# Second layer of a two-layer model: which operands of the scan's side work lie in PSUM, and which engine adds an epsilon

## Chip, cores and metric

One core of a Trainium2 chip runs the whole program. The metric is device time in microseconds (us), the median of the runs. Engines are named as in the profile: PE multiplies matrices, DVE is the vector engine, ACT the scalar engine (functions by table), POOL the general one, and SP issues DMAs. Everything is float32.

## What is computed

The reference is a two-layer network on `x` of shape (4, 2048, 256). The first layer (an RWKV-like recurrence with a feed-forward part, then experts) is not touched. The second layer is a selective scan (Mamba-like) and then two groups of 32 experts, of which each token takes two in each group. Cut to what the change touches:

```python
# selective scan, d_inner = 512, d_state = 16, per token t (x here is layer-normalised)
x_ssm, res = split(x @ W_in.T)            # 512 and 512 columns
x_ssm = silu(conv4(x_ssm) + b_conv)
B_C   = x_ssm @ W_x.T                     # the second 16 columns
dt    = softplus(x_ssm @ W_dt.T + b_dt)   # the "step size"; its logits are x_ssm @ W_dt.T + b_dt
h     = exp(dt * A) * h + dt * B * x_ssm  # 512 x 16 states, one step per token
y     = (h.sum(-1) + D * x_ssm) * silu(res)
x     = x + y @ W_out.T
# experts, for each of two groups of 32 (on layernorm(x), eps 1e-5)
scores = softmax(xn @ router_w); w, idx = top_k(scores, 2)
out   += 0.5 * sum over the picks of w * expert[idx](xn)
```

## The kernel before

The 8192 tokens go through the second layer in 16 chunks of 512. `layer1_phase` (from L939) writes out one order of work for all engines. Its backbone is `scans` (L1341): 64 steps per chunk, one for each of 4 blocks `e` of 128 inner columns and each of 16 states `n`. In step `g`, POOL computes `dbx = dtx * B` for two states at a time (L1368), ACT computes `exp(A*dt)` into one of three PSUM banks (L1375), DVE runs the recurrence of step `g-2` over 512 tokens with one scan instruction (L1386, result `hs`), and PE transposes `hs` of step `g-3` and adds it up in PSUM (L1402). `dbx` has room for 6 steps and `hs` for 8.

After each step the loop pulls side work a little further (`background.pull`). The side work is written as generators: each `yield` ends a slot, and a stream advances by `rate` slots per step. Three streams run beside the scans of chunk `c`:

- `before(c + 1)`, rate 1.15: normalise (L998), transpose, input product, convolution (L1119), SiLU (L1128), gates (L1148), the product for B, and at the end `step_size(e)` for four blocks (L1164): PE makes the logits (L1167), ACT copies them with their bias into `dt` in SBUF (L1175) and makes `ln(1 + exp(-|z|))` in `tmp` (L1176, L1179, L1181), DVE adds `max(z, 0)` (L1184) and multiplies by `xs` to get `dtx` (L1188).
- `after_scan(c - 1)`, rate 1.15: transpose of the gated output, product with `W_out` in two halves, each with its sum into `xb` (L1233), normalise, transpose, `router` (L1457), then ranks and places of the picks (L1257 to L1308).
- `sort_rows(c - 1)`, rate 0.4: indirect DMAs that POOL issues (L1325).

Every engine runs its instructions in the order written. Three PSUM banks (`G = Banks(psum, 0, 3)`) serve both streams in turn; `claim` skips a bank whose last user has not yet been written out ("held"), and PE waits for the mark in `G.freed` before it writes the bank again.

`normalise` takes mean and variance on DVE (L1003, L1006), adds the epsilon on DVE (L1008), raises to -0.5 on POOL (L1011), and makes the shift on DVE (L1014):

```python
m = dve.mark(nc.vector.tensor_scalar(rstd[:, :], mv[:, :, 1], EPS_LN, None, ALU.add))
yield from pause(POOL_LAG)
pool.after(m)
```

`router` handles 8 rows per partition (4 tiles, 2 groups) of 32 experts. ACT copies the scores from PSUM to `prob` (L1473); DVE takes the peak (L1478) and subtracts it (L1480); ACT applies exp (L1484); DVE sums (L1488), inverts (L1490), and divides all 256 values (L1492), picks the largest (L1496) and their indices (L1502), turns these to float (L1507), and compares them with `iota` into `onehot` (L1509), whose sum is `chosen` (L1513).

Of the kernel before, what the change touches and what calls it, by code (L numbers as in the profile page):

```python
# [5 lines left out]
P = 128  # L6
# [204 lines left out]
def layer0_phase(nc, psum, consts, I, L, sems, x_in, x_out, second_layer):  # L211
# [6 lines left out]
    with ExitStack() as st, ExitStack() as scanning:  # L218
# [51 lines left out]
        ssq, eps_gn, eps_rms = sb("ssq", [P, TL]), sb("eps_gn", [P, 1]), sb("eps_rms", [P, 1])  # L270
# [668 lines left out]
def layer1_phase(nc, psum, consts, I, L, sems, Z, route_of, x_in, x_out):  # L939
# [7 lines left out]
    with ExitStack() as st, ExitStack() as early:  # L947
# [6 lines left out]
        ident, neghalf = consts["ident"], consts["neghalf"]  # L954
# [120 lines left out]
        def before(c):  # L1075
# [88 lines left out]
            def step_size(e):  # L1164
# [19 lines left out]
                m = m_done["tmp free", e % 2] = m_done["dt", c, e] = dve.mark(nc.vector.scalar_tensor_tensor(  # L1184
                    out=dt_[:, e, :], in0=dt_[:, e, :], scalar=0.0, in1=tmp[:, e % 2, :], op0=ALU.max, op1=ALU.add))
# [19 lines left out]
        def after_scan(c):  # L1205
# [14 lines left out]
            dve.engine.wait_ge(s_xb, c * 16 + 16)  # L1220
            for half in range(2):
# [7 lines left out]
                m = pe.mark(m)  # L1229
                yield from pause(LAG)  # L1230
# [22 lines left out]
            dve.mark(nc.vector.tensor_scalar(route.weights[:, part, :].rearrange("p t (g k) -> p (t g) k", g=GR), R["best"][:, :, 0:TOP], 0.5, None, ALU.mult))  # L1253
# [203 lines left out]
def router(nc, L, G, xT, W_router, R, iota, groups, experts, top, lag=1):  # L1457

# [6 lines left out]
    rows = TL * groups  # L1465
    i, bank = yield from G.claim(pe)
# [11 lines left out]
    m = dve.mark(nc.vector.tensor_reduce(R["peak"][:, :], R["prob"][:, :, :], mybir.AxisListType.X, ALU.max))  # L1478
    dve.after(m)
    m = dve.mark(nc.vector.tensor_tensor(R["prob"][:, :, :], R["prob"][:, :, :], R["peak"][:, :].unsqueeze(2).broadcast_to([P, rows, experts]), ALU.subtract))  # L1480
    for _ in range(lag):
        yield
    act.after(m)
    m = act.mark(nc.scalar.activation(R["prob"][:, :, :], R["prob"][:, :, :], ACT.Exp))  # L1484
    for _ in range(lag):
        yield
    dve.after(m)
    m = dve.mark(nc.vector.tensor_reduce(R["total"][:, :], R["prob"][:, :, :], mybir.AxisListType.X, ALU.add))  # L1488
    dve.after(m)
    m = dve.mark(nc.vector.reciprocal(R["total"][:, :], R["total"][:, :]))  # L1490
    dve.after(m)
    m = dve.mark(nc.vector.tensor_tensor(R["prob"][:, :, :], R["prob"][:, :, :], R["total"][:, :].unsqueeze(2).broadcast_to([P, rows, experts]), ALU.mult))  # L1492
    yield
# [13 lines left out]
    m = dve.mark(nc.vector.tensor_copy(R["index_f"][:, :, :], R["index"][:, :, 0:top]))  # L1507
    dve.after(m)
    m = dve.mark(nc.vector.tensor_tensor(R["onehot"][:, :, :, :], iota[:, 0:experts].unsqueeze(1).unsqueeze(1).broadcast_to([P, rows, top, experts]),  # L1509
                                         R["index_f"][:, :, :].unsqueeze(3).broadcast_to([P, rows, top, experts]), ALU.is_equal))  # L1510
# [537 lines left out]
```

## Time and profile before

| | |
|---|---|
| median of 3 runs | 5326.36 us (5324.19 to 5327.82) |
| profiled execution | 5320.49 us, of which its span 5318.7 us |
| mean granted TensorE clock | 0.918 of full |
| busy over the span | PE 84%, DVE 74%, POOL 57%, ACT 49% |
| second layer with its scans | about 2680 to 4600 us of the span |

The span is the time from the first to the last instruction. A "group" below is all instructions of one line and form; behind its count stand the busy us of the group and the mean ns of one, then the idle us of the engine just before them and who ended it.

### The profile page before, as it was taken

Reading aid. Unit: us, or ns where it says so; the run is one execution under the profiler, and the core shown is the slowest. Engines: PE = TensorE matmul, PEld = TensorE weight load, DVE = VectorE, ACT = ScalarE, POOL = GpSimd, SP = SyncE. Lnnn points to the kernel's source line nnn. Section 1 sums busy time; section 2 is a strip of 40 time slices with the busy share of each in tenths; the row PEclk is TensorE's granted clock in tenths of the full one; section 3 lists DMA queues with packets and bytes.
Section 4 is the critical chain, followed back from the end, with each engine's and each line's share of the span. In section 5 each row is a group of like instructions: output and inputs, shape, how many; then the busy total and the mean of one; then the engine's idle time right before and its main releaser. Section 6 shows DMA issues by size and latency. Waiting matters only on the chain.

```text
span 5318.7 us, 58348 instructions
## 1 busy us (share of the span) xinstructions
PE 4466.3 (84%) x18832; PEld 2897.8 (54%) x18832; DVE 3946.1 (74%) x6263; ACT 2597.7 (49%) x4829; POOL 3016.0 (57%) x1940
## 2 busy tenths in 40 slices
PE   4788989888898888899978888888888888489994
PEld 1344555555555555566655555555555555378773
DVE  5977677676776767675078998898999888645676
ACT  1244344434433444444566666666666666244442
POOL 2445444445543445453167778777777777645552
PEclk8799999999999999999988899989988898699997
DMA  3223232323332233332121111111212111386777
GB/s 120 88 99 101 91 99 84 97 86 103 107 97 76 91 96 95 101 102 84 48 81 52 68 60 60 60 60 61 77 70 72 61 61 62 146 235 195 240 247 266
DMA packets 302654, 545.49 MB, mean 103 GB/s; under 512 B 30736, under 2 KB 146704, under 8 KB 293392
## 3 DMA queue, kind: packets, MB, share of 16 engines
q1 hardware_dynamic: 274704, 466.10, 27.0%
q0 software_dynamic: 27648, 75.67, 3.9%
q8 instruction: 153, 2.51, 0.2%
q14 instruction: 149, 1.22, 0.1%
HBM read 422.73 MB, written 118.92 MB: 102 GB/s over the span
## 4 chain that ended last, share of the span: by engine, by line
PE 50%; DVE 25%; ACT 9%; issue 7%; POOL 6%; DMA 2%; SPq 0%; DVEq 0%; POOLq 0%; another core or an unknown queue 0%; ACTq 0%
PE psum L207 21%; DVE c_hs L1386 7%; PE psum L1856 5%; PE psum L762 5%; DVE a_S L857 4%; PE psum L646 4%; POOL c_dbx L1368 4%; PE psum L1119 4%; PE psum L1402 3%; DVE a_prod L863 3%; PE psum L1879 3%; PE psum L1841 1%; PE psum L879 1%; ACT L770 1%; POOL sorted_rows L1325 1%
## 5 line engine op out<-in xcount | busy, mean ns | idle before, releaser
L1368 POOL TENSOR_TENSOR c_dbx<-c_dtx,c_Brep 128x1024 f32<-128x1024 f32 x512 | 1211.5, 2377 | 399.9 <-DVE c_hs L1386 328.0
L848 POOL TENSOR_TENSOR a_kv<-a_rk,a_kv 128x512 f32<-128x512 f32 x512 | 764.8, 1507 | 564.5 <-DMA a_kv<-v_rows 564.3
L1386 DVE TENSOR_TENSOR_SCAN c_hs<-psum,c_carry,c_dbx 128x512 f32<-128x512 f32 x768 | 931.6, 1262 | 47.2 <-ACT psum L1375 40.5
L1375 ACT ACTIVATE psum<-c_dt,c_cols 128x512 f32<-128x512 f32 x1024 | 698.2, 689 | 473.1 <-DVE c_hs L1386 469.3
L1402 PE MATMUL psum<-ident,c_hs 128*128 128x128 f32 x4096 | 703.1, 311 | 261.6 <-DVE c_hs L1386 252.5
L781 POOL TENSOR_TENSOR a_hid_e<-a_hid_e,a_g_rep 128x512 f32<-128x512 f32 x256 | 381.4, 1493 | 825.5 <-ACT a_hid_e L770 617.8
L1402 PEld LDWEIGHTS psum<-ident,c_hs 128*128 128x128 f32 x4096 | 540.8, 159 | 557.3 <-DVE c_hs L1386 395.0
L857 DVE TENSOR_TENSOR_SCAN a_S<-a_decay,a_carry,a_kv 128x513 f32<-128x513 f32 x512 | 785.7, 1535 | 38.7 <-POOL a_kv L848 33.9
L207 PE MATMUL psum<-a_xT,a_W_up 128*128 128x512 f32 x1152 | 579.6, 634 | 67.1 <-ACT a_hid_e L770 66.8
L863 DVE TENSOR_TENSOR a_prod<-a_rk,a_S 128x512 f32<-128x512 f32 x512 | 513.9, 1004 | 124.9 <-PE psum L879 124.8
L762 PE MATMUL psum<-a_W_down,a_hid_e 128*128 128x256 f32 x2304 | 552.4, 385 | 17.0 <-POOL a_hid_e L781 17.0
L762 PEld LDWEIGHTS psum<-a_W_down,a_hid_e 128*128 128x128 f32 x2304 | 438.7, 193 | 199.0 <-issue 108.1
L1768 POOL DMA_INDIRECT results<-d_ys,d_to_row x320 | 312.4, 976 | 276.5 <-issue 121.8
L207 PEld LDWEIGHTS psum<-a_xT,a_W_up 128*128 128x128 f32 x1152 | 222.8, 200 | 292.8 <-issue 186.4
L770 ACT ACTIVATE a_hid_e<-psum 128x512 f32<-128x512 f32 x288 | 170.5, 596 | 360.9 <-PE psum L207 359.9
L1856 PE MATMUL psum<-d_w,d_xT 128*128 x1280 | 333.8, 384 | 3.6 <-issue 3.1
L1386 DVE TENSOR_TENSOR_SCAN c_hs<-psum,c_dbx 128x512 f32<-128x512 f32 x256 | 295.0, 1201 | 34.8 <-ACT psum L1375 27.1
L1325 POOL DMA_INDIRECT sorted_rows<-route_xn,route_to_row x256 | 269.8, 1054 | 63.1 <-issue 45.5
L207 PE MATMUL psum<-a_xT,a_w 128*128 128x256 f32 x1024 | 248.4, 390 | 13.4 <-ACT a_hid_f L654 11.9
L1167 PE MATMUL psum<-c_xs,c_W_dt 128*128 128x512 f32 x512 | 246.8, 606 | 0.0
L646 PE MATMUL psum<-a_w,a_hid_f 128*128 128x256 f32 x1024 | 240.6, 381 | 4.7 <-ACT a_hid_f L654 4.7
L1871 DVE TENSOR_TENSOR d_h<-d_h,psum 128x128 f32<-128x128 f32 x320 | 91.8, 287 | 205.0 <-ACT d_h L1867 145.8
(265 smaller groups left out, 7343.0 us busy)
## 6 DMA issues: line engine op xcount, KB each, us to landing
a_kv<-v_rows SPq DMA_DIRECT2D x512, 256.0 KB
a_g_rep<-g_rows SPq DMA_DIRECT2D x256, 256.0 KB, 3.7
c_Brep<-b_rows SPq DMA_DIRECT2D x64, 1024.0 KB, 4.7
d_xs<-sorted_rows SPq DMA_DIRECT2D x320, 128.5 KB
d_w<-results SPq DMA_DIRECT2D x64, 512.0 KB, 11.5
d_w<-in_d_experts SPq DMA_DIRECT2D x32, 768.0 KB
sorted_rows<-d_zeros SPq DMA_DIRECT2D x66, 128.5 KB, 3.8
a_xa<-in_L_attn_x SPq DMA_DIRECT2D x16, 512.0 KB, 4.7
```

Of the source, the lines that this page charges most:

```text
L207: last = nc.tensor.matmul(out, lhsT, rhs, start=(n == 0), stop=(n == len(pairs) - 1))
L646: m_down = nc.tensor.matmul(sums[:, t * D:(t + 1) * D], hid_f[:, r, s * HALF + t * P:s * HALF + (t + 1) * P], w2[:, 2 * (f - 1) + s, :], s ...
L762: m_down = nc.tensor.matmul(banks[t // 2][1][:, (t % 2) * D:(t % 2 + 1) * D], hid_e[:, r, t * P:(t + 1) * P], W_down[:, q, :], start=(q == ...
L781: hid[e - 1] = m_done["gate used", n] = pool.mark(nc.gpsimd.tensor_tensor(hid_e[:, r, :], hid_e[:, r, :], g_rep[:, n % NG, :], ALU.mult))
L848: m_kv[g] = pool.mark(nc.gpsimd.tensor_tensor(kv[:, g % NV, 1:C + 1], rk[slot][:, 1, hb, :], kv[:, g % NV, 1:C + 1], ALU.mult))
L857: m_scan[q] = dve.mark(nc.vector.tensor_tensor_scan(S[:, q % NS, :], decay[cq % 2][:, hb, :], kv[:, q % NV, :], carry[:, sq_:sq_ + 1], ALU ...
L863: m_prod[q] = dve.mark(nc.vector.tensor_tensor(prod[:, q % NP, :], rk[cq % 2][:, 0, sq_ // DK, :], S[:, q % NS, 0:C], ALU.mult))
L1368: m_dbx[g] = m_dbx[g + 1] = pool.mark(nc.gpsimd.tensor_tensor(dbx[:, r:r + 2, :], dtx[slot][:, e, :].unsqueeze(1).broadcast_to([P, 2, C]), ...
L1375: m_da[g] = act.mark(nc.scalar.activation(psum[:, DA + g % ND, :], dt[slot][:, e, :], ACT.Exp, scale=A[:, e, n:n + 1]))
L1386: m_scan[q] = dve.mark(nc.vector.tensor_tensor_scan(hs[:, q % NR, :], psum[:, DA + q % ND, :], dbx[:, q % NX, :], first, ALU.mult, ALU.add))
L1402: last = nc.tensor.matmul(psum[:, YB + e % 2, t * P:(t + 1) * P], hs[:, q % NR, t * P:(t + 1) * P], ident[:, :], is_transpose=True, start= ...
L1856: m = nc.tensor.matmul(bank[:, 0:2 * P], xT[:, q % N3, kb * P:(kb + 1) * P], w[:, bass.ds(at_w[q] + kb * 2 * P, 2 * P)], start=(kb == 0), ...
```

## The change

Six edits, all but the first two inside `before`, `after_scan` and `router`:

1. A constant tile `eps` is shared by both layers (the first layer's `eps_gn` becomes this tile; what it holds is the same).
2. In the second layer's `normalise`, ACT adds the epsilon instead of DVE, two slots after the variance; POOL's power comes one slot later than before.
3. The step logits with their bias stay in their PSUM bank (ACT rewrites them there, after the absolute value) until DVE reads them for the sum; the bank is free after that sum and not after ACT's second reading.
4. In `router`, there is no copy by ACT: DVE reads the scores from the PSUM bank. The probabilities are not divided by their sum; the weights of the picks are multiplied by the inverse sum instead. The indices of the picks are written as floats into the same bank beside the scores, and the one-hot comparison reads them there. The bank is free after that comparison.
5. The two products with `W_out` are issued in two banks, and both sums follow.
6. The wait for `xb` moves from before the products to before the sums.

```diff
@@ normalise
-            dve.after(m)
-            m = dve.mark(nc.vector.tensor_scalar(rstd[:, :], mv[:, :, 1], EPS_LN, None, ALU.add))
-            yield from pause(POOL_LAG)
+            yield from pause(LAG)
+            act.after(m)
+            m = act.mark(nc.scalar.activation(rstd[:, :], mv[:, :, 1], ACT.Identity, bias=eps[:, 0:1]))
+            yield from pause(POOL_LAG - 1)
@@ step_size
-                m_z = act.mark(nc.scalar.activation(dt_[:, e, :], bank, ACT.Identity, bias=b_dt[:, e, :]))
-                m = G.freed[i] = act.mark(nc.scalar.activation(tmp[:, e % 2, :], bank, ACT.Abs, bias=b_dt[:, e, :]))
+                act.mark(nc.scalar.activation(tmp[:, e % 2, :], bank, ACT.Abs, bias=b_dt[:, e, :]))
+                m = m_z = act.mark(nc.scalar.activation(bank, bank, ACT.Identity, bias=b_dt[:, e, :]))
...
-                m = m_done["tmp free", e % 2] = m_done["dt", c, e] = dve.mark(nc.vector.scalar_tensor_tensor(
-                    out=dt_[:, e, :], in0=dt_[:, e, :], scalar=0.0, in1=tmp[:, e % 2, :], op0=ALU.max, op1=ALU.add))
+                dve.after(*scanned)
+                m = G.freed[i] = m_done["tmp free", e % 2] = m_done["dt", c, e] = dve.mark(nc.vector.scalar_tensor_tensor(
+                    out=dt_[:, e, :], in0=bank, scalar=0.0, in1=tmp[:, e % 2, :], op0=ALU.max, op1=ALU.add))
@@ after_scan
-            dve.engine.wait_ge(s_xb, c * 16 + 16)
+            products = []
             for half in range(2):
                 i, bank = yield from G.claim(pe)
...
-                m = pe.mark(m)
-                yield from pause(LAG)
+                products.append((i, bank, pe.mark(m)))
+                yield
+            yield from pause(LAG)
+            dve.engine.wait_ge(s_xb, c * 16 + 16)
+            for half, (i, bank, m) in enumerate(products):
                 dve.after(m)
...
-            dve.mark(nc.vector.tensor_scalar(route.weights..., R["best"][:, :, 0:TOP], 0.5, None, ALU.mult))
+            dve.after(m)
+            dve.mark(nc.vector.scalar_tensor_tensor(out=route.weights..., in0=R["best"][:, :, 0:TOP], scalar=0.5,
+                                                    in1=R["total"][:, :].unsqueeze(2).broadcast_to([P, TL * GR, TOP]), op0=ALU.mult, op1=ALU.mult))
@@ router
-    for _ in range(lag - 1):
+    scores = bank[:, 0:TL * NE].rearrange("p (r e) -> p r e", e=experts)
+    picks = bank[:, TL * NE:TL * NE + rows * top].rearrange("p (r k) -> p r k", k=top)
+    for _ in range(lag + 1):
         yield
-    act.after(m)
-    m = act.mark(nc.scalar.copy(R["prob"]..., bank[:, 0:TL * NE]))
-    G.freed[i] = m
-    for _ in range(lag):
-        yield
     dve.after(m)
-    m = dve.mark(nc.vector.tensor_reduce(R["peak"], R["prob"], X, ALU.max))
+    m = dve.mark(nc.vector.tensor_reduce(R["peak"], scores, X, ALU.max))
     dve.after(m)
-    m = dve.mark(nc.vector.tensor_tensor(R["prob"], R["prob"], R["peak"] broadcast, ALU.subtract))
+    m = dve.mark(nc.vector.tensor_tensor(prob, scores, R["peak"] broadcast, ALU.subtract))
...
-    m = dve.mark(nc.vector.reciprocal(R["total"], R["total"]))
-    dve.after(m)
-    m = dve.mark(nc.vector.tensor_tensor(R["prob"], R["prob"], R["total"] broadcast, ALU.mult))
-    yield
-    dve.after_alone(m)
...
-    m = dve.mark(nc.vector.tensor_copy(R["index_f"], R["index"][:, :, 0:top]))
-    dve.after(m)
-    m = dve.mark(nc.vector.tensor_tensor(R["onehot"], iota broadcast, R["index_f"] broadcast, ALU.is_equal))
+    m = dve.mark(nc.vector.tensor_copy(picks, R["index"][:, :, 0:top]))
+    dve.mark(nc.vector.tensor_copy(R["index_f"], R["index"][:, :, 0:top]))
+    dve.mark(nc.vector.reciprocal(R["total"], R["total"]))
+    dve.after(m)
+    m = G.freed[i] = dve.mark(nc.vector.tensor_tensor(R["onehot"], iota broadcast, picks broadcast, ALU.is_equal))
```

(The indices of some views are shortened here. In `router` the instructions for the largest values now follow the sum in its slot.)

## Rows read from the trace of the kernel before

**Rows 1.** Timeline of DVE, first and last of 12 one-hot comparisons: start, length (us)
```profile
2857.14 2.89 DVE L1509 TENSOR_TENSOR c_onehot<-c_iota,c_index_f 128x512 f32<-128x512 f32 x1
...
4192.21 2.90 DVE L1509 TENSOR_TENSOR c_onehot<-c_iota,c_index_f 128x512 f32<-128x512 f32 x1
```

**Rows 2.** Windows view: stretch, length, busy us of each engine, TensorE clock, DMA
```profile
3225.00:3289.00 64.00, 47.03 (x234) 32.06 (x233) 63.12 (x71) 41.08 (x74) 48.50 (x26) 0.89 0.24 91
3289.00:3326.00 37.00, 36.94 (x176) 23.88 (x175) 29.37 (x33) 21.96 (x38) 35.05 (x19) 1.00 0.14 47
3326.00:3344.00 18.00, 16.42 (x62) 8.09 (x61) 13.95 (x38) 15.87 (x23) 10.27 (x7) 0.91 0.05 18
```

**Rows 3.** Chain of waits in one chunk: start us, length us, what
```profile
3285.07 0.66 PE psum L1402 x4
...
3324.33 1.75 PE psum L207 x16
...
3326.10 0.37 ACT c_prob L1473
...
3327.78 1.26 ACT c_xs L1128 x2
```

**Rows 4.** Groups of DVE instructions, 2450 to 4600 us
```profile
L1184 DVE SCALAR_TENSOR_TENSOR c_dt<-c_dt,c_tmp 128x512 f32<-128x512 f32 x64 | 83.4, 1302 | 42.8 <-ACT c_tmp L1181 42.7
L1188 DVE TENSOR_TENSOR c_dtx<-c_dt,c_xs 128x512 f32<-128x512 f32 x64 | 71.9, 1124 | 1.1
L1014 DVE SCALAR_TENSOR_TENSOR c_shift<-c_mv,c_rstd 128x4 f32<-128x4 f32 x31 | 46.6, 1502 | 1.1 <-POOL c_rstd L1011 1.1
...
L1509 DVE TENSOR_TENSOR c_onehot<-c_iota,c_index_f 128x512 f32<-128x512 f32 x15 | 39.4, 2624 | 0.5
L1008 DVE TENSOR_SCALAR c_rstd<-c_mv 128x4 f32<-128x4 f32 x31 | 36.8, 1186 | 1.1
L1492 DVE TENSOR_TENSOR c_prob<-c_prob,c_total 128x256 f32<-128x256 f32 x15 | 30.3, 2021 | 0.5
...
L1233 DVE TENSOR_TENSOR c_xb<-c_xb,psum 128x512 f32<-128x512 f32 x30 | 20.6, 687 | 40.0 <-PE psum L207 40.0
...
L1480 DVE TENSOR_TENSOR c_prob<-c_prob,c_peak 128x256 f32<-128x256 f32 x15 | 16.4, 1092 | 0.5
...
L1304 DVE SCALAR_TENSOR_TENSOR c_place<-c_index_f,c_place 128x16 f32<-128x16 f32 x15 | 9.2, 614 | 0.5
...
L1478 DVE TENSOR_REDUCE c_peak<-c_prob 128x8 f32<-128x256 f32 x15 | 6.3, 418 | 59.4 <-ACT c_prob L1473 59.4
```

**Rows 5.** Timeline of POOL, then of DVE, where the one-hot comparison starts
```profile
3344.29 2.34 POOL L1368 TENSOR_TENSOR c_dbx<-c_dtx,c_Brep 128x1024 f32<-128x1024 f32 x1 [0.25 <-DVE c_index_f L1507]
...
3344.30 2.88 DVE L1509 TENSOR_TENSOR c_onehot<-c_iota,c_index_f 128x512 f32<-128x512 f32 x1
```

**Rows 6.** Timeline of DVE at the step sizes of one chunk
```profile
3357.74 0.73 DVE L1184 SCALAR_TENSOR_TENSOR c_dt<-c_dt,c_tmp 128x512 f32<-128x512 f32 x1
...
3371.29 2.47 DVE L1184 SCALAR_TENSOR_TENSOR c_dt<-c_dt,c_tmp 128x512 f32<-128x512 f32 x1
3373.80 0.69 DVE L1188 TENSOR_TENSOR c_dtx<-c_dt,c_xs 128x512 f32<-128x512 f32 x1
...
3377.95 1.89 DVE L1184 SCALAR_TENSOR_TENSOR c_dt<-c_dt,c_tmp 128x512 f32<-128x512 f32 x1
```

**Rows 7.** Timeline of PE, then of DVE, behind the router's product
```profile
3328.52 5.40 PE L207 MATMUL psum<-c_W_in,c_xT 128*128 128x512 f32 x8 [1.58 <-ACT c_xs L1128]
...
3331.08 3.63 DVE L1386 TENSOR_TENSOR_SCAN c_hs<-psum,c_carry,c_dbx 128x512 f32<-128x512 f32 x3 [2.51 <-ACT psum L1375]
```

**Rows 8.** Groups of ACT instructions, 2450 to 4600 us
```profile
L1375 ACT ACTIVATE psum<-c_dt,c_cols 128x512 f32<-128x512 f32 x1024 | 698.2, 689 | 473.1 <-DVE c_hs L1386 469.3 <-issue 1.3
...
L332 ACT ACTIVATE a_rstd<-a_mv,a_eps_gn 128x4 f32<-128x4 f32 x1 | 0.3, 297 | 0.0
```

**Rows 9.** Timeline of PE at the third step-size product
```profile
3356.87 1.88 PE L1167 MATMUL psum<-c_xs,c_W_dt 128*128 128x512 f32 x4
```

More of the change, by code:

```diff
@@ L269, in layer0_phase @@
         ln_rstd, ln_shift = small("ln_rstd"), small("ln_shift")
-        ssq, eps_gn, eps_rms = sb("ssq", [P, TL]), sb("eps_gn", [P, 1]), sb("eps_rms", [P, 1])
+        ssq, eps_gn, eps_rms = sb("ssq", [P, TL]), consts["eps"], sb("eps_rms", [P, 1])
         R = router_buffers(nc, st, "a", 1, E, TOP)
@@ L953, in layer1_phase @@
         s_load, s_rest, s_xa, s_xb, s_store, s_bout = (sem(n) for n in ("load", "rest", "xa", "xb", "store", "bout"))
-        ident, neghalf = consts["ident"], consts["neghalf"]
+        ident, neghalf, eps = consts["ident"], consts["neghalf"], consts["eps"]
         norm = [None, None]
@@ L1252, in after_scan @@
             dve.mark(nc.vector.tensor_scalar(xn_[:, :, D], token_row[:, :], float(c * C * TOP), None, ALU.add))
-            dve.mark(nc.vector.tensor_scalar(route.weights[:, part, :].rearrange("p t (g k) -> p (t g) k", g=GR), R["best"][:, :, 0:TOP], 0.5, None, ALU.mult))
+            dve.after(m)
+            dve.mark(nc.vector.scalar_tensor_tensor(out=route.weights[:, part, :].rearrange("p t (g k) -> p (t g) k", g=GR), in0=R["best"][:, :, 0:TOP], scalar=0.5,
+                                                    in1=R["total"][:, :].unsqueeze(2).broadcast_to([P, TL * GR, TOP]), op0=ALU.mult, op1=ALU.mult))
             ahead = route.ahead
@@ L1465, in router @@
     rows = TL * groups
+    prob, best = R["prob"], R["best"]
     i, bank = yield from G.claim(pe)
@@ L1469, in router @@
     m = pe.mark(m)
-    for _ in range(lag - 1):
+    scores = bank[:, 0:TL * NE].rearrange("p (r e) -> p r e", e=experts)
+    picks = bank[:, TL * NE:TL * NE + rows * top].rearrange("p (r k) -> p r k", k=top)
+    for _ in range(lag + 1):
+        yield
+    dve.after(m)
+    m = dve.mark(nc.vector.tensor_reduce(R["peak"][:, :], scores, mybir.AxisListType.X, ALU.max))
+    dve.after(m)
+    m = dve.mark(nc.vector.tensor_tensor(prob[:, :, :], scores, R["peak"][:, :].unsqueeze(2).broadcast_to([P, rows, experts]), ALU.subtract))
+    for _ in range(lag):
         yield
     act.after(m)
-    m = act.mark(nc.scalar.copy(R["prob"][:, :, :].rearrange("p r e -> p (r e)"), bank[:, 0:TL * NE]))
-    G.freed[i] = m
+    m = act.mark(nc.scalar.activation(prob[:, :, :], prob[:, :, :], ACT.Exp))
     for _ in range(lag):
@@ L1477, in router @@
     dve.after(m)
-    m = dve.mark(nc.vector.tensor_reduce(R["peak"][:, :], R["prob"][:, :, :], mybir.AxisListType.X, ALU.max))
-    dve.after(m)
-    m = dve.mark(nc.vector.tensor_tensor(R["prob"][:, :, :], R["prob"][:, :, :], R["peak"][:, :].unsqueeze(2).broadcast_to([P, rows, experts]), ALU.subtract))
-    for _ in range(lag):
-        yield
-    act.after(m)
-    m = act.mark(nc.scalar.activation(R["prob"][:, :, :], R["prob"][:, :, :], ACT.Exp))
-    for _ in range(lag):
-        yield
-    dve.after(m)
[L1488 to L1493, printed above, removed]
-    dve.after_alone(m)
+    m_total = dve.mark(nc.vector.tensor_reduce(R["total"][:, :], prob[:, :, :], mybir.AxisListType.X, ALU.add))
     for r in range(rows):
-        m = dve.mark(nc.vector.max(R["best"][:, r, :], R["prob"][:, r, :]))
+        m = dve.mark(nc.vector.max(best[:, r, :], prob[:, r, :]))
         if r == rows // 2 - 1:
@@ L1501, in router @@
     for r in range(rows):
-        m = dve.mark(nc.vector.max_index(R["index"][:, r, :], R["best"][:, r, :], R["prob"][:, r, :]))
+        m = dve.mark(nc.vector.max_index(R["index"][:, r, :], best[:, r, :], prob[:, r, :]))
         if r == rows // 2 - 1:
@@ L1505, in router @@
     yield
+    dve.after(m, m_total)
+    m = dve.mark(nc.vector.tensor_copy(picks, R["index"][:, :, 0:top]))
+    dve.mark(nc.vector.tensor_copy(R["index_f"][:, :, :], R["index"][:, :, 0:top]))
+    dve.mark(nc.vector.reciprocal(R["total"][:, :], R["total"][:, :]))
     dve.after(m)
[L1507 to L1510, printed above, removed]
+    m = G.freed[i] = dve.mark(nc.vector.tensor_tensor(R["onehot"][:, :, :, :], iota[:, 0:experts].unsqueeze(1).unsqueeze(1).broadcast_to([P, rows, top, experts]),
+                                                      picks.unsqueeze(3).broadcast_to([P, rows, top, experts]), ALU.is_equal))
     dve.after(m)
@@ L1927, in build @@
         consts = {"ident": st.enter_context(nc.sbuf_tensor("ident", [P, P], F32)),
+                  "eps": st.enter_context(nc.sbuf_tensor("eps", [P, 1], F32)),
                   "neghalf": st.enter_context(nc.sbuf_tensor("neghalf", [P, 4], F32))}
```

## The prediction

> **What bounds the kernel now.** I read the page's slices first: the second layer shows a DVE that is nearly always busy, beside a PE that is hardly less so. To part the two I took the timeline of DVE and looked for an instruction that comes once per chunk. The one-hot comparison does; 12 of them span 11 chunks, (4192.21 - 2857.14) / 11 = 121.4 us each [rows 1]. Then I cut one chunk with the windows view [rows 2]. It has three stages, and each has another limit:
>
> - A, 64 us, from the one-hot comparison to the first sum into `xb`: DVE is busy 63.12 of 64, PE 47.03. DVE sets the time here.
> - B, 37 us, up to the router's product: PE is busy 36.94 of 37, DVE 29.37. PE sets the time, and what DVE saves here is worth nothing.
> - C, 18 us, up to the next comparison: no engine is full (PE 16.42, ACT 15.87, DVE 13.95). The three wait for each other.
>
> The chain of waits agrees: from 3285.07 it runs over PE to the end of the router's product at 3326.08, goes over to ACT's copy of the scores (3326.10, 0.37 us) and from there to the SiLU that stands behind this copy in ACT's order [rows 3]. DVE's peak (L1478) stood 59.4 us in 15 chunks waiting for that copy [rows 4].
>
> Then I read DVE's groups for instructions that take longer than their size [rows 4]. A 128x512 sum with one operand in PSUM (L1233) takes 687 ns. The comparison has the same size and both operands in SBUF, and takes 2624. L1184 takes 1302, L1188 1124, the division L1492 2021, and L1008 1186 for four columns. The timeline shows why: POOL starts a `dbx` at 3344.29 that lasts to 3346.63, the comparison starts 0.01 us later and lasts 2.88, so that it ends 0.55 us after POOL [rows 5]. It stood while POOL ran. The 30 sums with a PSUM operand average 0.687, so they show no such wait.
>
> The Trainium skill (SBUF — State Buffer, section Who interferes with whom) states this as a lock: a DVE instruction with two SBUF inputs, or one in a two-port mode, and a GpSimd instruction that reads SBUF exclude each other for the whole instruction. The trace agrees, with 2.88 against 0.69 us. The same rule speaks against the change at one place: L1188 keeps two SBUF inputs, so it can inherit what L1184 no longer waits. If all four step sizes passed it on, that edit would bring nothing, and the sum below would be 1.2 us per chunk (18 us in all) smaller.
>
> **The change, part by part**, in us per chunk; 15 chunk times carry both side streams.
>
> One-hot comparison: 2.62 falls to 0.69, the row of a PSUM operand: 1.93. Behind it stand a scan, a reduction and short work, about 2.6 us, by which time the `dbx` has ended. All of it lies in A and counts.
>
> Epsilon of the incoming chunk: L1008 leaves DVE in A, 1.19. ACT gets the nearest row's 0.30 [rows 8]; ACT stands idle 473 us before its exponentials in this stretch, which hides it. Were ACT full it would cost 2 x 0.30. The variance is written two slots ahead, so nothing is queued behind a wait; POOL's power comes a slot later, and `before` has some 68 of 73.6 slots filled, so it still ends in time. The second epsilon (for `xb`) lies in B: nothing.
>
> Step sizes: 4 x (1.30 - 0.69) = 2.44 of waiting in L1184, all in A. Where `dtx` follows directly, it takes the wait over: at 3371.29 L1184 took 2.47 and L1188 behind it 0.69 [rows 6]. Where a scan lies between, as after 3377.95, POOL has ended. The bounds are 0 and 2.44; the rows show about one of each kind, so I take half, 1.22. ACT's rewriting into PSUM costs what its PSUM-writing exponentials do, 0.69 [rows 8], the size of the instruction it replaces: nothing.
>
> Router, entry (C): ACT no longer stands behind the scores. Its SiLU and exponentials run while PE works. PE waited 1.58 for that SiLU at 3328.52, and DVE 2.51 for the exponential at 3331.08 [rows 7]. The lower bound is 1.58. The upper is 2.51 + 0.37, when DVE and not PE sets C. I take PE's 1.58 and the copy's 0.37, 1.95, since PE is the fuller engine in C.
>
> Router, division: L1492 (2.02) and the wait in L1480 (1.09 - 0.42, by the peak's row of the same size: 0.67) go. Between 0 and 2.69; C has other limits than DVE, so I take 0.
>
> Output halves: DVE's 40 us of waiting in L1233, 1.33 each, lie where PE is full. They go, and nothing comes of it. The wait for `xb` moves with them; its load is issued before the transposes, so it is covered as before.
>
> Added on DVE: a second copy of the indices, and weights with two SBUF inputs. The nearest row is L1304 (128x16, two SBUF inputs), 0.61 with its waits. Each is between nothing and 0.61; I take 0.4 for both, and at most 1.2.
>
> Banks: the router holds one of three for 11 slots, and each step size holds one until DVE's sum. The third step size would take the first one's bank: PE began it at 3356.87 [rows 9], while L1184 of the first ran from 3357.74 to 3358.47 [rows 6]. That is 1.6 of waiting, in A, where PE has 17 us of idle time. I take 0; the bound is 1.6.
>
> Sum: A 1.93 + 1.19 + 1.22 = 4.34; C 1.95; less 0.4; 5.9 per chunk, times 15 = 88 us. From the profiled 5320.5 that makes 5232; the median of the runs shown lies 5.9 above the profiled execution: **5238**. Low end: 1.93 + 1.19 + 0 + 1.58 - 1.2 - 1.6 = 1.9, 28 us. High end: 1.93 + 1.19 + 2.44 + 2.88 + 2.69 = 11.1, 167 us.
>
> **Rivals.**
>
> 1. The waiting is handed on. L1188 or L1014 (1502 ns for four columns [rows 4]) stands against POOL instead, or scans come up against `dbx`, since DVE and POOL then both run dense. POOL's 48.50 of 64 in A speaks against the latter; rows 6 speak for the former in part. A then keeps only about half of the one-hot and epsilon parts, 1.6, and C its 1.95, less 0.4: 3.1, or 47 us, 5279.
> 2. C becomes DVE's own. With ACT ahead and the division gone, 1.2 of the 2.69 counts, C gives 2.3 in place of 1.95, and the step sizes pass on nothing: 5.9 + 1.2 + 0.35 + 1.22 = 8.7 per chunk, 130 us, 5196. For it: DVE idles 2.51 beside PE's 1.58. Against: PE has only 1.6 us of room in C.
> 3. PE bounds the whole chunk. It is busy about 100 of 121 us, and the granted clock is 0.89 in A against 1.00 in B [rows 2]; if what A gives is lost again at the clock, the time stays at 5326. Against: PE has 17 us of idle time in A.
> 4. Slower: two banks do not suffice. The place is B and C, where PE is full: the gate and B products must then wait for ACT's evacuation of a bank that it used one or two products ago. One such wait costs about the 1.58 of rows 7. It decides from four per chunk (5.9 / 1.58); with five, 8 us, the change costs 2 per chunk, 32 us, 5358. Against: the SiLU that frees each bank is no longer held up by the scores.
>
> **How the numbers follow.** Forecast 0.52 (own range 5215 to 5262), rival 1 0.22, rival 2 0.14, rival 3 0.05, rival 4 0.07. A measurement of this kernel can tell about 0.2%, some 11 us. Faster is the first three, 0.88; the same 0.05; slower 0.07. The range 5185 to 5300 leaves out rivals 3 and 4 and the far ends of 1 and 2, about 0.18 together.
>
> **What the profile would show.** The comparison near 0.69 us, L1184's successor near 0.69 in all 64, its `dtx` between 0.7 and 1.7 on average; a chunk time near 115.5; stage B still 37 us; a peak that waits for PE and not for ACT; no PE idle time at the gates' product. Wrong would be shown by PE waits on DVE's sum or on a SiLU in B or C, by a longer `dtx` group than 72 + 40 us of busy time, or by an unchanged A with shorter DVE instructions and more idle time on DVE.

## The result, and the profile after

The changed kernel takes 5201.66 us (median of 4 runs, 5199.28 to 5204.73) against 5325.27 before: ratio 0.9768, 95% interval 0.9753 to 0.9782. That is 124 us less, where 88 were forecast (5238 us). The time is also 13 us below the forecast's own range of 5215 to 5262, and nearest to the 5196 us of rival 2. Its profiled execution has a span of 5197.5 us.

The one-hot comparison marks the chunks as before. These are the first and the last of 12 in the timeline of DVE after the change (start, length):

```profile
2855.91 0.63 DVE L1508 TENSOR_TENSOR c_onehot<-c_iota,psum 128x512 f32<-128x512 f32 x1
...
4104.69 0.64 DVE L1508 TENSOR_TENSOR c_onehot<-c_iota,psum 128x512 f32<-128x512 f32 x1
```

(4104.69 - 2855.91) / 11 = 113.5 us per chunk, against 121.4 [rows 1]. So a chunk gives 7.8 us, and not 5.9. The comparison itself now takes 0.63 us in place of 2.89 (2.62 on average before).

The stages of one chunk in the windows view after (stretch, length, busy us of PE, PE's weight loads, DVE, ACT and POOL, TensorE clock, DMA share, GB/s), which answer to [rows 2]:

```profile
3196.00:3260.00 64.00, 53.21 (x253) 37.44 (x252) 62.42 (x75) 46.57 (x82) 53.40 (x28) 0.84 0.27 97
3260.00:3295.00 35.00, 33.48 (x164) 21.79 (x163) 30.23 (x31) 22.53 (x38) 30.20 (x16) 1.00 0.11 38
3295.00:3310.00 15.00, 14.59 (x65) 7.82 (x64) 11.87 (x35) 12.12 (x19) 10.29 (x7) 1.00 0.07 21
```

In A DVE is still the fullest (62.42 of 64), but PE has grown from 47.03 to 53.21 and POOL from 48.50 to 53.40. In B PE is no longer full: 33.48 of 35, where it was 36.94 of 37. C takes 15 us in place of 18 with PE at 14.59.

In A the granted clock has fallen from 0.89 to 0.84.

These windows are cut where one chunk happens to stand. A is 64 us long in both, in part because its end is the first sum into `xb`, and edit 5 has moved that sum behind both products: over 11 chunks it comes 65.8 us after the comparison in the kernel before, 64.6 in the changed one, and 62.8 in the changed one without edits 5 and 6 (u_halves, below). For the balance I averaged 11 chunks, by the starts of four instructions in the timeline of DVE:

| from ... to | before | after | difference |
|---|---|---|---|
| comparison ... statistics of the incoming chunk | 44.03 | 40.50 | -3.53 |
| ... statistics of `xb` | 29.63 | 28.01 | -1.62 |
| ... peak of the scores | 29.45 | 30.00 | +0.55 |
| ... next comparison | 18.26 | 15.01 | -3.25 |
| chunk | 121.37 | 113.52 | -7.85 |

The norm has one slot more and the router one fewer. So a scan has moved from the fourth part (8 scans before, 7 after) to the third, and these two are read together: -2.70. The first two, in which DVE is the fullest, give -5.15. In the third PE is still nearly full by these averages, busy for 29.4 of 30.0 us where it was 29.0 of 29.5; the 33.48 of 35 above is one chunk, and takes in the end of the second part.

The DVE groups after that answer to [rows 4], from 2450 to 4480 us, which again hold 15 routers, and the two new small instructions (L1259 the weights, L1504 the picks):

```profile
L1190 DVE TENSOR_TENSOR c_dtx<-c_dt,c_xs 128x512 f32<-128x512 f32 x64 | 82.1, 1282 | 0.1
L1015 DVE SCALAR_TENSOR_TENSOR c_shift<-c_mv,c_rstd 128x4 f32<-128x4 f32 x31 | 71.2, 2295 | 4.8 <-POOL c_rstd L1012 4.8
...
L1186 DVE SCALAR_TENSOR_TENSOR c_dt<-psum,c_tmp 128x512 f32<-128x512 f32 x64 | 42.4, 663 | 46.7 <-ACT c_tmp L1182 46.6
...
L1238 DVE TENSOR_TENSOR c_xb<-c_xb,psum 128x512 f32<-128x512 f32 x30 | 19.8, 672 | 17.7 <-PE psum L207 17.7
...
L1508 DVE TENSOR_TENSOR c_onehot<-c_iota,psum 128x512 f32<-128x512 f32 x15 | 9.5, 634 | 0.0
...
L1257 DVE TENSOR_SCALAR route_xn<-c_token_row 128x4 f32<-128x4 f32 x15 | 7.1, 474 | 0.0
L1483 DVE TENSOR_TENSOR c_prob<-psum,c_peak 128x256 f32<-128x256 f32 x15 | 6.4, 424 | 0.5
L1481 DVE TENSOR_REDUCE c_peak<-psum 128x8 f32<-128x256 f32 x15 | 6.3, 421 | 39.7 <-PE psum L207 39.7
...
L1311 DVE SCALAR_TENSOR_TENSOR c_place<-c_index_f,c_place 128x16 f32<-128x16 f32 x15 | 4.6, 307 | 0.5
...
L1259 DVE SCALAR_TENSOR_TENSOR route_weights<-c_best,c_total 128x16 f32<-128x16 f32 x15 | 2.7, 178 | 0.0
...
L1504 DVE CAST psum<-c_index 128x16 f32<-128x16 uint32 x15 | 2.4, 159 | 0.0
```

The sum of the step size (L1186) has the length of its size, 0.66 us, in all 64. But its product L1190 went from 1.12 to 1.28, and the shift L1015 from 1.50 to 2.30: part of the waiting was handed on. To see how much, take for the instructions that [rows 4] show to be longer than their size, and for the row numbers of the tokens (L1252 before), the busy time less its count times the shortest it can take (0.66 us for 128x512, 0.42 for 128x256, 0.15 to 0.17 for the small ones). I call this DVE's waiting, and take it from 2450 to 4600 us. It leaves out two small casts, of the indices and of the places, which wait as well: 1 and 2 us before, 2 and 2 after. Before it is 217 us (step sum 41, product 30, shift 42, comparison 30, epsilon 32, division 24, subtraction 10, places 7, token rows 3). After it is 113, of which 66 in the shift and 40 in the product.

Behind the router's product, the rows that answer to [rows 7], of PE, DVE and ACT in the timeline after:

```profile
3297.94 1.88 PE L207 MATMUL psum<-c_W_in,c_xT 128*128 128x512 f32 x4
...
3299.99 2.46 DVE L1393 TENSOR_TENSOR_SCAN c_hs<-psum,c_carry,c_dbx 128x512 f32<-128x512 f32 x2 [2.42 <-ACT psum L1382]
...
3297.27 0.69 ACT L1129 ACTIVATE c_xs<-psum,c_cols 128x512 f32<-128x512 f32 x1 [4.66 <-PE psum L1120]
3297.98 1.28 ACT L1382 ACT_TABLE_LOAD   x1
```

PE's gate product no longer waits (it stood 1.58 us). DVE still does, 2.42 us for an exponential. ACT stands ahead of that with a SiLU (L1129) that waits 4.66 us for the convolution, which PE now finishes only behind the router's product. Behind the SiLU ACT also loads a table for 1.28 us before the exponential can start. ACT was freed from one wait and met the next one.

### The profile page after: what moved, and what is told of

It reads as the page before. It is cut to its first block, busy times and chain, and to the rows that moved or that the text cites. A ratio compares the mean times of both kernels' runs of the same rounds, so it can differ in the third digit from the quotient of the medians.

```text
span 5197.5 us, 58292 instructions
## 1 busy us (share of the span) xinstructions
PE 4433.8 (85%) x18832; PEld 2891.8 (56%) x18832; DVE 3826.1 (74%) x6231; ACT 2617.9 (50%) x4859; POOL 3006.2 (58%) x1940
## 3 DMA queue, kind: packets, MB, share of 16 engines
q14 instruction: 149, 1.22, 0.1%
## 4 chain that ended last, share of the span: by engine, by line
PE 52%; DVE 20%; ACT 10%; POOL 8%; issue 6%; DMA 2%; SPq 0%; DVEq 0%; POOLq 0%; another core or an unknown queue 0%; ACTq 0%
PE psum L207 22%; POOL c_dbx L1375 5%; PE psum L1855 5%; PE psum L762 5%; DVE a_S L857 4%; DVE c_hs L1393 4%; PE psum L646 4%; PE psum L1120 4%; PE psum L1409 4%; DVE a_prod L863 3%; PE psum L1878 3%; PE psum L1840 2%; POOL sorted_rows L1332 1%; PE psum L879 1%; PE psum L1168 1%
## 5 line engine op out<-in xcount | busy, mean ns | idle before, releaser
L1409 PE MATMUL psum<-ident,c_hs 128*128 128x128 f32 x4096 | 686.1, 306 | 211.4 <-DVE c_hs L1393 206.1
L1409 PEld LDWEIGHTS psum<-ident,c_hs 128*128 128x128 f32 x4096 | 530.3, 156 | 480.9 <-DVE c_hs L1393 327.3
L207 PEld LDWEIGHTS psum<-a_xT,a_w 128*128 128x128 f32 x1024 | 200.0, 197 | 80.0 <-issue 23.3
```

Of the source, the lines that this page charges most:

```text
L207: last = nc.tensor.matmul(out, lhsT, rhs, start=(n == 0), stop=(n == len(pairs) - 1))
L1409: last = nc.tensor.matmul(psum[:, YB + e % 2, t * P:(t + 1) * P], hs[:, q % NR, t * P:(t + 1) * P], ident[:, :], is_transpose=True, start= ...
```

## The experiments

Four kernels are the one before with one part of the change alone, two split the router further, three take one edit of the full change back or away, one changes POOL's instruction size, and two go beyond the change. Each ratio is to the kernel before on the same chip. "Chunk" and "waiting" are read as above.

| kernel | ratio (95%) | chunk | DVE's waiting |
|---|---|---|---|
| before | 1 | 121.4 | 217 |
| p_step: edit 3 alone | 0.9945 (0.9932 to 0.9959) | 119.6 | 188 |
| p_router: edit 4 alone | 0.9902 (0.9886 to 0.9917) | 118.0 | 194 |
| r_scores: of edit 4, no copy by ACT | 0.9934 (0.9918 to 0.9949) | 118.7 | 208 |
| r_picks: of edit 4, picks in PSUM | 0.9953 (0.9940 to 0.9966) | 119.2 | 190 |
| p_eps: edit 2 alone | 1.0004 (0.9995 to 1.0014) | 122.0 | 165 |
| p_halves: edits 5 and 6 alone | 0.9951 (0.9938 to 0.9965) | 120.5 | 179 |
| full change | 0.9768 (0.9753 to 0.9782) | 113.5 | 113 |
| u_halves: full, edits 5 and 6 taken back | 0.9772 (0.9759 to 0.9785) | 112.9 | 101 |
| u_eps: full, edit 2 taken back | 0.9825 (0.9812 to 0.9837) | 116.0 | 118 |
| s_slot: u_eps with a slot more | 0.9817 (0.9803 to 0.9830) | 115.3 | 129 |
| x_single: before, POOL by single states | 0.9986 (0.9976 to 0.9996) | 121.6 | 192 |
| n_shift: full, shift off DVE | 0.9722 (0.9709 to 0.9736) | 111.7 | 47 |
| n_both: n_shift, step size in PSUM for dtx | 0.9683 (0.9670 to 0.9696) | 110.0 | 7 |

### Step logits in PSUM, alone (p_step)

The `step_size` part of the diff above, and nothing else.

> Before with edit 3 alone (step logits stay in PSUM until DVE's sum). Port theory (DVE with two SBUF inputs stands while POOL runs): the sum falls from 1.30 to 0.66 us in all 64, the product behind it takes over about a quarter of it, 1.8 us per chunk are left, 27 us: ratio 0.995. Rival (the wait is handed on whole to the product dtx): sum at 0.66, product from 1.12 to about 1.76 us, ratio 1.000. Rival (banks held longer stop PE): ratio above 1.002, PE waits on DVE's sum.

Its DVE groups, product and sum:

```profile
L1189 DVE TENSOR_TENSOR c_dtx<-c_dt,c_xs 128x512 f32<-128x512 f32 x64 | 81.6, 1275 | 1.1
...
L1185 DVE SCALAR_TENSOR_TENSOR c_dt<-psum,c_tmp 128x512 f32<-128x512 f32 x64 | 43.0, 672 | 42.8 <-ACT c_tmp L1181 42.7
```

The sum falls to 0.67. The product rises by 0.15, so that of the 40 us of waiting that the sums lost, 10 came back in it. 1.8 us per chunk are left, as expected here; the prediction had taken 1.22. That the rows of one chunk showed as many pairs that hand the wait on as pairs that don't made me take half; over all 64 it is a quarter. PE now waits for a bank until DVE's sum, 5.0 us in 5 waits between 2850 and 4100 us, where the prediction's bound was 1.6 per chunk; the ratio shows nothing of it.

### The router's edits, alone and split (p_router, r_scores, r_picks)

p_router has the whole `router` of the change and the new weights. r_scores takes only this of it:

```diff
-    m = act.mark(nc.scalar.copy(R["prob"][:, :, :].rearrange("p r e -> p (r e)"), bank[:, 0:TL * NE]))
-    G.freed[i] = m
...
-    m = dve.mark(nc.vector.tensor_tensor(R["prob"][:, :, :], R["prob"][:, :, :], R["peak"]...
+    m = G.freed[i] = dve.mark(nc.vector.tensor_tensor(R["prob"][:, :, :], scores, R["peak"]...
```

and r_picks only this:

```diff
-    G.freed[i] = m
...
+    m = dve.mark(nc.vector.tensor_copy(picks, R["index"][:, :, 0:top]))
...
+    m = G.freed[i] = dve.mark(nc.vector.tensor_tensor(R["onehot"]..., picks.unsqueeze(3)..., ALU.is_equal))
```

> Before with edit 4 alone (router: no copy by ACT, no division, picks in PSUM, weights with the inverse sum). Port theory with ACT freed from the copy: the comparison falls from 2.62 to 0.63 us (2.0 per chunk) and the stage between router and comparison gives 2 to 3 us: 4 to 5 us per chunk, 60 to 75 us, ratio 0.987. Rival (the gain comes only from DVE's shorter instructions in the DVE-bound stage): 30 us, ratio 0.994. Rival (the router's bank, held for 11 slots, costs PE): below 30 us, with PE waits on SiLU.

> Before with only the copy by ACT removed (DVE reads the scores from PSUM, the bank is free after the subtraction; division and comparison as before). My sum gives 1.95 us per chunk in the stage behind the router, 29 us, ratio 0.9945: no PE idle time before the gates' product. Rival (the gain of the router's edits is DVE's alone, from comparison and division): ratio 0.999 to 1.000.

> Before with only the comparison's picks in PSUM (a second small copy, the bank held until the comparison). The prediction's sum: comparison 2.62 to 0.63 us, 1.9 per chunk, 29 us, ratio 0.9945. Rival (handed on): the next instruction with a two-port mode or two SBUF inputs (the row numbers of the tokens, 0.36 us before, and the places, 0.61) takes it over, as both did in the router's edits together (1.68 and 1.85): 0 to 5 us, ratio 0.999 to 1.000.

p_router gave 52 us (0.0098 of 5317), less than expected. Its DVE groups show where the rest went, places, token rows and comparison:

```profile
L1306 DVE SCALAR_TENSOR_TENSOR c_place<-c_index_f,c_place 128x16 f32<-128x16 f32 x16 | 29.6, 1851 | 0.6
L1252 DVE TENSOR_SCALAR route_xn<-c_token_row 128x4 f32<-128x4 f32 x16 | 26.9, 1681 | 0.0
...
L1503 DVE TENSOR_TENSOR c_onehot<-c_iota,psum 128x512 f32<-128x512 f32 x16 | 10.2, 634 | 0.0
```

The comparison is free of its wait, but two instructions behind it, which stand against POOL like it, took it over: token rows from 0.36 to 1.68 us, places from 0.61 to 1.85. Together that is 42 us of new waiting.

Yet r_picks alone gave 25 us, and there token rows and places stayed at 0.37 and 0.61. So that the comparison's wait is handed on is no property of the edit. I take it to depend on where the streams stand against POOL when all edits of a kernel are in. In the full change token rows are at 0.47 and places at 0.31, and hardly anything is handed on at that place.

r_scores gave 35 us (0.0066 of 5283); the part between peak and comparison fell from 18.26 to 15.74. That is the step on ACT of the prediction, and somewhat more than its 1.95. In this kernel and in p_router PE no longer waits for the SiLU (15.8 us in 10 waits before, between 2850 and 4100 us), so the expected rivals, a gain of DVE's alone and a bank that costs PE, did not come true. The two parts add to 60 us, against 52 for the whole router. Dropping the division was not tried alone, and what it adds does not show beside what was handed on; the prediction had put it at 0.

### The epsilon (p_eps, u_eps, s_slot)

p_eps is the `normalise` part of the diff with the shared constant; u_eps is the full change without that part; s_slot is u_eps with one more slot:

```diff
-            yield from pause(POOL_LAG)
+            yield from pause(POOL_LAG + 1)
             pool.after(m)
```

> Before with edit 2 alone (ACT adds the epsilon of the second layer's norms; power and shift one slot later). Port theory as predicted: 1.19 us of the incoming chunk's norm count, 18 us, ratio 0.9965. Rival (the wait goes on to the shift, two SBUF inputs, 1.50 us before and 2.30 in the full change): shift above 2 us, ratio 0.999 to 1.000.

> The full change with the epsilon back on DVE (edit 2 taken back, slots as before). Alone it gave 1.0004. If its wait is handed on to the shift in any order of work: ratio 0.977 as in the full change, shift back near 1.5 us. Rival (it pays once the other edits have made DVE's order fixed): ratio 0.980.

> The full change with the epsilon back on DVE but the power one slot later, as with ACT's epsilon. Slot theory: what edit 2 brings in the full change (0.9768 against 0.9825 without it) is the slot, which puts other PE work ahead of the transposes that wait for ACT's normalised rows (19.8 us of PE waiting in ten chunks without it, none with it): ratio 0.978 to 0.979. Rival (it is the instruction taken off DVE, 1.16 us): ratio 0.982 to 0.983.

Alone the edit gave nothing, with the shift's group at

```profile
L1015 DVE SCALAR_TENSOR_TENSOR c_shift<-c_mv,c_rstd 128x4 f32<-128x4 f32 x31 | 61.2, 1973 | 5.3 <-POOL c_rstd L1012 5.1
```

that is 1.97 us in place of 1.50. This is less than the rival had named (above 2), and of the 32 us that the epsilon lost, the shift took 15 over. Still DVE's waiting as a whole fell by 52 us (44, if the cast of the indices is counted, which rose from 0.22 to 0.79 us), and the time did not follow. Much of that fall is in the router, where nothing was edited: the division went from 2.02 to 0.60 us, and the comparison is at

```profile
L1510 DVE TENSOR_TENSOR c_onehot<-c_iota,c_index_f 128x512 f32<-128x512 f32 x15 | 10.4, 693 | 0.5
```

PE's waits between 2850 and 4100 us show two that grew (waiting instruction and who ended it: us, times, longest):

```profile
PE psum L207 <- DVE route_ahead L1261: 24.2, 11, 2.2
PE psum L207 <- ACT c_xs L1129: 22.2, 11, 2.0
```

The wait for `route_ahead` was not in that list before at all, and the one for `c_xs` was 15.8. But the largest, for `hs`, fell from 148.8 to 119.6, and all in the list together from 183 to 170. What grew is PE's busy time: from 2680 to 4560 us it is 1609 us against 1582, with about as many matmuls (7323 against 7336) and at a lower granted clock (0.87 against 0.89). So it is PE's longer work and not its waiting that stands against DVE's gain. Why it was longer was not tried.

In the full change the same edit is worth 0.9825 - 0.9768 = 0.0057, 30 us. My first thought was the slot that comes with it, since without the edit PE stands before the transposes of the normalised rows (same view, u_eps):

```profile
PE psum L1036 <- ACT route_xn L1018: 19.8, 10, 3.4
```

s_slot has the slot without the edit. That wait is gone from its list, and the ratio is 0.9817, within the interval of u_eps. The slot theory falls. What was on record as its rival, the instruction taken off DVE, is left. s_slot and the full change have the same slots and differ in the epsilon's engine, and by the averages over 11 chunks the second part of the chunk goes from 28.82 to 28.01 and the third from 31.00 to 30.00, with the other two unchanged. So both epsilons count, the one for `xb` too. In the third part PE is busy for 29.8 of 31.0 us in s_slot and 29.4 of 30.0 in the full change: with the epsilon on DVE it had 1.2 us of room there.

### Both halves, then both sums (p_halves, u_halves)

The `after_scan` part of the diff alone, and the full change without it.

> Before with edits 5 and 6 alone (both output products, then both sums, the wait for xb behind the products). As predicted: DVE's waits of 1.33 us at the sums lie where PE is full, so ratio 1.000 although these waits shrink. Rival (they count: up to 2.7 us per chunk, 40 us): ratio 0.992.

> The full change with edits 5 and 6 taken back (each output half with its sum at once). Alone these edits gave 0.9951, against my step that DVE's waits at the sums cost nothing because PE is full there. Theory of PE order: what counts is that the second product need not stand behind DVE's first sum in the slot order, so that PE and the norm start earlier; taking it back costs about 25 us here too, ratio 0.981 to 0.982. Rival, phase: alone the edits only moved DVE's two-input instructions against POOL's (the comparison fell to 0.69 us without PSUM), which PSUM operands already give in the full change; then the ratio stays at 0.977 to 0.978.

The prediction had said that nothing comes of this edit. Alone it gives 26 us. Its DVE groups, token rows and comparison:

```profile
L1255 DVE TENSOR_SCALAR route_xn<-c_token_row 128x4 f32<-128x4 f32 x15 | 28.8, 1920 | 0.0
...
L1512 DVE TENSOR_TENSOR c_onehot<-c_iota,c_index_f 128x512 f32<-128x512 f32 x15 | 10.4, 692 | 0.5
```

The comparison reads SBUF as before and takes 0.69 us: the other order has moved it away from POOL's instructions. The token rows took 1.6 us of that over. The division lost its wait in the same way (2.02 to 0.62). DVE's waits at the sums fell too, from 40.0 to 19.5 us. Against that PE stands at the transposes of the normalised rows (waits of p_halves, 2850 to 4100 us):

```profile
PE psum L1036 <- ACT route_xn L1018: 18.6, 10, 3.4
```

In the full change the edit is worth nothing: 0.9772 without it and 0.9768 with it. This is what the rival on phase had said, that the gain alone came at places that operands in PSUM make safe anyway. It is argued and not shown, and p_eps speaks against a simple form of it: there too the comparison (0.69) and the division (0.60) lost their waits and the token rows took some over (1.85), and nothing was gained. The chunk average gives 0.9 us, or 14 of the 26; the rest lies outside the 11 chunks. How much of the gain came from the comparison and how much from the sums is not settled.

### POOL's instruction half as long (x_single)

```diff
-                        m_dbx[g] = m_dbx[g + 1] = pool.mark(nc.gpsimd.tensor_tensor(
-                            dbx[:, r:r + 2, :], dtx[slot][:, e, :].unsqueeze(1).broadcast_to([P, 2, C]), Brep[:, n:n + 2, :], ALU.mult))
+                        for k in range(2):
+                            m_dbx[g + k] = pool.mark(nc.gpsimd.tensor_tensor(
+                                dbx[:, r + k:r + k + 1, :], dtx[slot][:, e, :].unsqueeze(1).broadcast_to([P, 1, C]), Brep[:, n + k:n + k + 1, :], ALU.mult))
```

> Before with POOL's product dbx issued for one state at a time (two instructions of 512 columns for one of 1024; the work is the same). Port theory: DVE's two-input instructions stand until the POOL instruction under way has ended, so halving that instruction about halves the excess: comparison from 2.62 to about 1.7 us, the sum of the step size from 1.30 to about 1.0, shift from 1.50 to about 0.9. Rival (the excess is the SBUF operand's own slowness): these stay as they were. The time: DVE gains up to 6 us per chunk, POOL pays two starts for one; between 0.985 and 1.01.

DVE's step sum, shift and comparison, then POOL's group:

```profile
L1184 DVE SCALAR_TENSOR_TENSOR c_dt<-c_dt,c_tmp 128x512 f32<-128x512 f32 x64 | 65.6, 1025 | 42.7 <-ACT c_tmp L1181 42.6
L1014 DVE SCALAR_TENSOR_TENSOR c_shift<-c_mv,c_rstd 128x4 f32<-128x4 f32 x31 | 45.5, 1469 | 9.2 <-POOL c_rstd L1011 9.2
...
L1510 DVE TENSOR_TENSOR c_onehot<-c_iota,c_index_f 128x512 f32<-128x512 f32 x15 | 28.5, 1900 | 0.5
```

```profile
L1369 POOL TENSOR_TENSOR c_dbx<-c_dtx,c_Brep 128x512 f32<-128x512 f32 x1024 | 1302.4, 1302 | 305.2 <-DVE c_hs L1387 241.4 <-DVE c_best L1497 26.0 <-DMA c_Brep<-b_rows 17.0
```

The comparison went from 2.62 to 1.90 and the step sum from 1.30 to 1.03, though nothing was changed at them or their operands. The excess is a matter of POOL's instructions, and not of the SBUF operand. The division fell too, from 2.02 to 1.46. But the shift (1.47) and the product (1.12) did not move, and the epsilon (1.19 to 1.45) and the subtraction (1.09 to 1.46) rose. Where POOL's next instruction follows at once, two short ones can hold DVE as long as one long one, here (POOL, then the shift):

```profile
3149.59 2.50 POOL L1369 TENSOR_TENSOR c_dbx<-c_dtx,c_Brep 128x512 f32<-128x512 f32 x2
...
3149.59 2.54 DVE L1014 SCALAR_TENSOR_TENSOR c_shift<-c_mv,c_rstd 128x4 f32<-128x4 f32 x1
```

It is not always so: other shifts end behind the first of two (3392.50, 0.95 us). POOL pays 91 us more (1302 against 1212). The time falls by 0.14%.

### Beyond the change (n_shift, n_both)

n_shift moves the shift, the largest wait left, to ACT and POOL. n_both also keeps the step size itself in PSUM until `dtx` is made:

```diff
+            act.mark(nc.scalar.activation(shift[:, :], mv[:, :, 0], ACT.Copy, scale=-1.0))
...
-            dve.after(m)
-            m = dve.mark(nc.vector.scalar_tensor_tensor(out=shift[:, :], in0=mv[:, :, 0], scalar=-1.0, in1=rstd[:, :], op0=ALU.mult, op1=ALU.mult))
+            pool.after(m)
+            m = pool.mark(nc.gpsimd.tensor_tensor(shift[:, :], shift[:, :], rstd[:, :], ALU.mult))
...
-                    out=dt_[:, e, :], in0=bank, scalar=0.0, in1=tmp[:, e % 2, :], op0=ALU.max, op1=ALU.add))
+                    out=bank, in0=bank, scalar=0.0, in1=tmp[:, e % 2, :], op0=ALU.max, op1=ALU.add))
...
-                m_done["dtx", c, e] = dve.mark(nc.vector.tensor_tensor(dtx_[:, e, :], dt_[:, e, :], xs_[:, e, :], ALU.mult))
+                m_x = dve.mark(nc.vector.tensor_tensor(dtx_[:, e, :], bank, xs_[:, e, :], ALU.mult))
+                act.after(m_x, *scanned)
+                m = G.freed[i] = m_done["dt", c, e] = act.mark(nc.scalar.copy(dt_[:, e, :], bank))
```

> The full change with the shift off DVE: ACT negates the mean beside the epsilon, POOL multiplies right after its power. The shift is the largest waiting left on DVE (2.23 us each, 66 us in all). If DVE's waits in the stage before the incoming norm count in full: 2 us per chunk, 30 us, ratio 0.971; if the waiting is handed on once more, to dtx: 0.975 to 0.977, dtx above 1.5 us.

> As the run with the shift off DVE, and the step size too stays in PSUM until dtx is made (DVE sums in place, multiplies from the bank, ACT copies dt to SBUF): dtx falls from 1.28 to 0.66 us. Port theory: 2.5 us per chunk more, ratio 0.965 to 0.968. Rival (banks): the bank is held some three slots longer and PE waits for ACT's copy, ratio above the shift's alone.

n_shift takes 0.9722, 1.8 us per chunk less than the full change; the product stays at 1.28, so nothing was handed on. It is between the two numbers expected. n_both takes 0.9683, 5118 us beside 5283 on its chip, and is the fastest of all. Its product:

```profile
L1191 DVE TENSOR_TENSOR c_dtx<-psum,c_xs 128x512 f32<-128x512 f32 x64 | 42.7, 668 | 0.1
```

It takes 0.67 for a sum of 42.7 us in place of 82.1. The chunk gives 1.7 us more, where 2.5 were expected, and the ratio is just above the 0.965 to 0.968 expected. The rival of the banks did not come true: each bank is now held until ACT's copy behind the product, and PE waited 6.5 us for that copy in 11 chunks.

## Why the prediction was right, and where not

The time lay in the stated range of 5185 to 5300 us and the mechanism held, but the sum was too small: 5.9 us per chunk against 7.8. The terms were off in both directions, so that the sum is nearer the truth than several of its terms.

- **DVE stands while POOL runs**, and PSUM operands end it: shown by r_picks and p_step, which changed little but the operands, and by x_single, which changed only POOL. The trace before says the same. Take the 235 instructions of the epsilon, the shift, the step sum and its product, the subtraction, the division and the comparison (2450 to 4600 us): 64 began while POOL was idle, and not one of these took over 0.15 us more than its size; of the 136 that began during a `tensor_tensor` of POOL, 122 did.
- **Comparison, 1.93**: right. r_picks measured 2.2 per chunk; its 25 us are 1.7 for each of 15.
- **Step sizes, 1.22 as half of 2.44**: mis-sized. 1.8 per chunk; a quarter was handed on.
- **Behind the router, 1.95**: mis-sized. r_scores alone gave 2.7. In the full change the third and fourth part together gave 2.70, but 1.0 of this is the epsilon's, below. The mechanism, ACT no longer standing before the SiLU, was right; DVE's own wait for ACT did not go (2.42 us).
- **Added work on DVE, 0.4**: mis-sized. Picks and weights take 0.16 and 0.18 us, neither with a wait, and the weights took 0.17 before as well.
- **Epsilon, 1.19 in A and nothing in B**: wrong both ways. Alone it gave nothing. In the full change it gave 2.5 per chunk by the averages (30 us, or 2.0, by the ratio): 0.8 in the second part and 1.0 in the third, where the prediction had counted nothing (s_slot), and the other 0.7 with the slot, which the ratios do not show clear of noise.
- **Output halves, nothing**: right within the full change, wrong alone.
- **"In B, what DVE saves is worth nothing"** is the step that failed. It was read from 36.94 us of PE in 37, and holds so for the kernel before (29.0 of 29.5 in the third part, over 11 chunks). With the other edits in and the epsilon still on DVE, PE is busy for 29.8 of 31.0 us in the third part, and an instruction less on DVE gave 1.0 us there. That stage B would stay at 37 us failed with it: 35 in the window.
- **Rival 1** was true in part. The shift took over 0.8 us of each epsilon, 25 us in all, and the product 0.16 of each step sum.
- **Rival 2** named the nearest time (5196), but by another path. In the last part PE is busy for 14.6 of 15.0 us and DVE for 12.3, so C did not become DVE's own, and the step sizes did pass a quarter on.
- **Rival 3**: the granted clock fell in the window of A (0.84 against 0.89) but not over the whole (mean 0.922 against 0.918), and did not take back what A gave. The rival's "about 100 of 121 us" of PE is 100 of the 119 that the three windows cover; over 11 chunks it is 103 of 121.4.
- **Rival 4** (banks) did not happen. By the prediction it decides from four waits of 1.58 us per chunk. Between 2850 and 4100 us PE waited about once per chunk for the evacuation of the gates, 0.4 us at most, and p_step, which holds the step sizes' banks longer, gave its full part.

By ratios the four parts alone give 0.9945 x 0.9902 x 1.0004 x 0.9951 = 0.9803, and together 0.9768. The difference of 0.0035 is hardly more than the intervals of the five runs leave open (0.003 together). What is clear of them is that single edits are worth another amount in company, the epsilon 0.6% more and the halves 0.45% less. That each edit moves all that is behind it against POOL is my explanation, and not shown by a run of its own.

## What to carry to other kernels

Where DVE and POOL share a stretch, compare each DVE instruction with one of its size that has an operand in PSUM, and sum the excess. The sum says where waiting can be taken away, and not what time it gives: taking nearly all of it away (217 to 7 us, n_both) gave 165 us, p_eps lost 52 us of it for nothing, and r_scores gained 35 us with 9 us less of it, because it also freed ACT. An edit tried alone can be 0.5% off either way from what it is worth in the end. That an engine is full in one stage does not say that nothing can be gained there once other edits have changed the order of work.

## What the runs showed of the hardware

I had expected a DVE instruction to wait for one instruction of POOL at most. The timeline after, POOL's rows and then DVE's shift, shows more:

```profile
3273.48 1.07 POOL L1332 DMA_INDIRECT sorted_rows<-route_xn,route_to_row  x1 [0.20 <-issue]
3274.58 4.68 POOL L1375 TENSOR_TENSOR c_dbx<-c_dtx,c_Brep 128x1024 f32<-128x1024 f32 x2
...
3274.30 4.99 DVE L1015 SCALAR_TENSOR_TENSOR c_shift<-c_mv,c_rstd 128x4 f32<-128x4 f32 x1
```

The shift starts at 3274.30, before POOL's two products (3274.58 to 3279.26), while POOL issues a DMA. It ends at 3279.29, behind both of them: 4.99 us for four columns. From the profile I cannot tell whether the DMA's issue held it at its start. Another shift has no DMA beside it (POOL, then DVE):

```profile
3159.10 4.65 POOL L1375 TENSOR_TENSOR c_dbx<-c_dtx,c_Brep 128x1024 f32<-128x1024 f32 x2
...
3159.16 4.62 DVE L1015 SCALAR_TENSOR_TENSOR c_shift<-c_mv,c_rstd 128x4 f32<-128x4 f32 x1 [1.40 <-POOL c_rstd L1012]
```

It began 0.06 us behind the first product and ended behind the second, which started some 2.3 us after it. The Trainium skill (SBUF — State Buffer, section Who interferes with whom) says that whoever issues first gets the shared pair. For the first product the trace agrees, 0.06 us ahead of the shift. For the second it does not: the shift had begun 2.3 us earlier, and still stood through it.

ACT's rewriting of a bank in place costs nothing extra: 0.64 to 0.65 us in the four of one chunk after (3205.28 to 3223.69), beside 0.68 for the same activation from PSUM to SBUF before.
